# Expert weights read with 4 KB per partition instead of 1 KB and 2 KB rows, in a mixture-of-experts kernel

## The reference, cut to what matters

```python
xn = layernorm(x)                                   # 8192 tokens x 512
out = x + random_feature_attention(xn) + moe(xn)

# moe, E = 64 experts, CAP = 256 slots each, K = 8 experts per token, I = 256
dispatch[flat_e, pos_c] += tokens[tidx] * valid     # (64, 256, 512)
g = einsum('ech,ehi->eci', dispatch, gate_w)        # gate_w (64, 512, 256)
u = einsum('ech,ehi->eci', dispatch, up_w)          # up_w   (64, 512, 256)
expert_out = einsum('eci,eih->ech', silu(g) * u, down_w)   # down_w (64, 256, 512)
output[tidx] += expert_out[flat_e, pos_c] * weight
output += (silu(tokens @ sgate) * (tokens @ sup)) @ sdown  # the shared expert
```

## Time and profile before

| what | value |
|---|---|
| median of 3 runs | 1535.04 us (1531.94 to 1538.73) |
| the profiled execution, its own time | 1536.14 us |
| its span, first to last instruction | 1534.4 us |
| PE busy | 1405.3 us, 92% of the span |
| DVE, ACT, POOL busy | 863.6, 643.0, 538.4 us |
| DMA, mean over the span | 163 GB/s, 249.70 MB in 174406 packets |

### The profile page before, as it was taken

The page is one execution under the profiler, slowest core; times in us unless marked ns, Lnnn a source line. Parts: engine busy times, 40 slices in busy tenths (PEclk is TensorE's granted clock), DMA queues, the critical chain, the costliest instruction groups (busy, mean ns, idle before and its releaser), DMA issues.

```text
span 1534.4 us, 23572 instructions
## 1 busy us (share of the span) xinstructions
PE 1405.3 (92%) x7965; PEld 1179.7 (77%) x7965; DVE 863.6 (56%) x1700; ACT 643.0 (42%) x1004; POOL 538.4 (35%) x679
## 2 busy tenths in 40 slices
PE   7999999999999999999999978988898988889894
PEld 5677777777777777777778978887787888788783
DVE  6846565455654556555446655655565655555551
ACT  5321122211222112221145756666665656656562
POOL 2100000000000000000015776677767677677673
PEclk9999999999999999999999999999999999999997
DMA  7333122331223312232128988899898988988985
GB/s 252 124 120 115 61 74 96 114 114 55 78 96 114 114 48 84 96 114 87 47 73 243 277 242 234 235 247 250 227 253 230 256 237 228 270 215 235 259 230 64
DMA packets 174406, 249.70 MB, mean 163 GB/s; under 512 B 31268, under 2 KB 99880, under 8 KB 174376
## 3 DMA queue, kind: packets, MB, share of 16 engines
q1 hardware_dynamic: 145704, 177.99, 36.1%
q0 software_dynamic: 28672, 71.32, 20.7%
HBM read 177.88 MB, written 71.39 MB: 162 GB/s over the span
## 4 chain that ended last, share of the span: by engine, by line
PE 41%; DMA 28%; POOL 11%; issue 9%; DVE 8%; ACT 1%; POOLq 1%; SPq 0%; DVEq 0%
DMA out_dram<-outs,sidx 28%; PE pmm L994 8%; PE pmm L995 7%; PE pmm L996 7%; POOL out_dram L1362 5%; PE pout L994 4%; PE pout L995 4%; PE pout L996 4%; POOL sidx L1357 2%; PE plog L1062 2%; PE ptr L1006 2%; POOL earlier L1341 2%; PE pmm L1027 2%; DVE score L705 2%; POOL pool_sink L1288 2%
## 5 line engine op out<-in xcount | busy, mean ns | idle before, releaser
L994 PE MATMUL pmm<-xt_hi,proj_hi 128*128 128x256 f32 (+1 forms) x784 | 266.1, 339 | 3.9 <-DVE xt_lo L949 2.1
L1341 POOL TENSOR_TENSOR earlier<-earlier,chosen 128x64 bf16<-128x64 bf16 x64 | 28.5, 446 | 677.2 <-DVE chosen L734 673.4
L995 PE MATMUL pmm<-xt_lo,proj_hi 128*128 128x256 f32 (+1 forms) x784 | 256.8, 327 | 0.0
L996 PE MATMUL pmm<-xt_hi,proj_lo 128*128 128x256 f32 (+1 forms) x784 | 256.3, 327 | 0.0
L994 PE MATMUL pmm<-xt_hi,sgu_hi 128*128 128x256 f32 (+1 forms) x768 | 252.6, 329 | 0.1
L995 PE MATMUL pmm<-xt_lo,sgu_hi 128*128 128x256 f32 (+1 forms) x768 | 245.8, 320 | 0.0
L996 PE MATMUL pmm<-xt_hi,sgu_lo 128*128 128x256 f32 (+1 forms) x768 | 245.6, 320 | 0.0
L1362 POOL DMA_INDIRECT out_dram<-outs,sidx x128 | 216.4, 1691 | 33.9 <-issue 33.9
L448 ACT ACTIVATE feat<-pmm,ab 128x512 f32<-128x512 f32 x68 | 46.8, 689 | 386.3 <-PE pmm L1027 382.1
L994 PEld LDWEIGHTS pmm<-xt_hi,proj_hi 128*128 128x128 f32 x784 | 155.6, 199 | 26.2 <-issue 11.3
L1348 POOL DMA_INDIRECT xbuf<-rows,gidx x128 | 162.9, 1272 | 29.5 <-issue 28.5
(11 more groups left out here) (186 smaller groups left out, 2912.8 us busy)
## 6 DMA issues: line engine op xcount, KB each, us to landing
raw<-in_L_ffn_gate_w_dram SPq DMA_DIRECT2D x64, 512.0 KB
raw<-in_L_ffn_up_w_dram SPq DMA_DIRECT2D x64, 512.0 KB
raw<-in_L_ffn_down_w_dram SPq DMA_DIRECT2D x64, 512.0 KB
xbuf<-in_L_attn_x_dram SPq DMA_DIRECT2D x16, 1024.0 KB, 6.4
rows<-xn SPq DMA_DIRECT2D x16, 1024.0 KB, 4.2
outs<-in_L_attn_x_dram SPq DMA_DIRECT2D x32, 512.0 KB, 3.8
out_dram<-outs SPq DMA_DIRECT2D x32, 512.0 KB, 3.0
rows<-weight SPq DMA_DIRECT2D x16, 128.0 KB, 2.9
```

The costliest lines, as they stand in the source:

```text
L994: pe.matmul(psum, lh, rh, start=first and n == 0, stop=False)
L995: pe.matmul(psum, lh, rl, start=False, stop=False)
L996: ins = pe.matmul(psum, ll, rh, start=False, stop=final and n == len(pairs) - 1)
L1341: pool.tensor_tensor(after, earlier[b][:, j, :], chosen[:, j, :], ALU.add).then_inc(earlier_made, 1)
```

## The change

The weights of the 64 experts are laid into the partitions differently: partition `p` now gets rows `4p` to `4p+3` of gate and of up, and rows `2p` and `2p+1` of down. In DRAM these rows are neighbours, so that each partition takes one run of 4096 bytes per matrix, where it took four runs of 1024 (gate, up) or two of 2048 (down). The rest follows from that:

- the transposes of the tokens take every fourth column (`h:H:HB`, a step of 16 bytes) instead of 128 neighbouring ones, so that block `h` holds the token's columns `4p + h`;
- the columns of gate and up must come out so that output partition `q` of block `i` is column `2q + i`, since the down matrix holds rows `2q + i` in partition `q`. ACT and DVE therefore read `raw` with a step of 8 bytes (`egu_raw`) and write the high and low parts in neighbouring columns. The matmuls read what they read before;
- the shared expert keeps the old layout and gets a load function of its own.

The number and the order of the instructions, the waits and the bytes moved are the same on every engine.

```diff
+        egu_raw = [raw[b][:, 0:GU].rearrange("p (a q i) -> p a i q", q=P, i=IB) for b in range(2)]

             def load_gate_up(b, gate, up):
+                sp.dma_start(raw[b][:, 0:GU // 2], gate.rearrange("(p c) i -> p (c i)", p=P)).then_inc(
+                    gu_loaded[b], 16)
+                sp.dma_start(raw[b][:, GU // 2:GU], up.rearrange("(p c) i -> p (c i)", p=P)).then_inc(
+                    gu_loaded[b], 16)
+
+            def load_down(b, down):
+                sp.dma_start(raw[b][:, GU:], down.rearrange("(p c) h -> p (c h)", p=P)).then_inc(dn_loaded[b], 16)
+
+            def load_shared(b):
                 sp.dma_start(raw[b][:, 0:GU // 2].rearrange("p (c i) -> p c i", c=HB),
-                             gate.rearrange("(c p) i -> p c i", p=P)).then_inc(gu_loaded[b], 16)
+                             sgate_w.rearrange("(c p) i -> p c i", p=P)).then_inc(gu_loaded[b], 16)
...
             def gate_up_hi(e):
...
-                act.activation(egu_hi[e.b], raw[e.b][:, 0:GU], copy).then_inc(egu_hi_made, 1)
+                act.activation(egu_hi[e.b].rearrange("p (a i q) -> p a i q", i=IB, q=P), egu_raw[e.b],
+                               copy).then_inc(egu_hi_made, 1)
...
             def gate_up_lo(e):
                 dve.wait_ge(egu_hi_made, e.n + 1)
-                dve.tensor_tensor(egu_lo[e.b], raw[e.b][:, 0:GU], egu_hi[e.b].bitcast(F32),
+                dve.tensor_tensor(egu_lo[e.b].rearrange("p (a i q) -> p a i q", i=IB, q=P), egu_raw[e.b],
+                                  egu_hi[e.b].bitcast(F32).rearrange("p (a i q) -> p a i q", i=IB, q=P),
                                   ALU.subtract).then_inc(egu_lo_made, 1)
...
-                        ins = pe.transpose(ptr_e[:, h, c * P:(c + 1) * P], xe[e.b][:, c, h * P:(h + 1) * P],
+                        ins = pe.transpose(ptr_e[:, h, c * P:(c + 1) * P], xe[e.b][:, c, h:H:HB],
                                            ident[:])
```

More of the change, by code:

```diff
@@ L319, in load_gate_up @@
             def load_gate_up(b, gate, up):
+                sp.dma_start(raw[b][:, 0:GU // 2], gate.rearrange("(p c) i -> p (c i)", p=P)).then_inc(
[5 more added lines that the diff above has]
+            def load_shared(b):
                 sp.dma_start(raw[b][:, 0:GU // 2].rearrange("p (c i) -> p c i", c=HB),
-                             gate.rearrange("(c p) i -> p c i", p=P)).then_inc(gu_loaded[b], 16)
+                             sgate_w.rearrange("(c p) i -> p c i", p=P)).then_inc(gu_loaded[b], 16)
                 sp.dma_start(raw[b][:, GU // 2:GU].rearrange("p (c i) -> p c i", c=HB),
-                             up.rearrange("(c p) i -> p c i", p=P)).then_inc(gu_loaded[b], 16)
-            def load_down(b, down):
+                             sup_w.rearrange("(c p) i -> p c i", p=P)).then_inc(gu_loaded[b], 16)
                 sp.dma_start(raw[b][:, GU:].rearrange("p (c h) -> p c h", c=IB),
-                             down.rearrange("(c p) h -> p c h", p=P)).then_inc(dn_loaded[b], 16)
+                             sdown_w.rearrange("(c p) h -> p c h", p=P)).then_inc(dn_loaded[b], 16)
             def store_xn(g):
@@ L378, in _ @@
             sp.dma_start(router_raw, router_w.rearrange("(c p) e -> p c e", p=P)).then_inc(router_loaded, 16)
-            load_gate_up(0, sgate_w, sup_w)
-            load_down(0, sdown_w)
+            load_shared(0)
             sp.wait_ge(consts_made, 1)
```

## The result

| | before | after |
|---|---|---|
| median | 1533.79 us, 20 runs (1529.08 to 1543.63) | 1542.41 us, 20 runs (1531.89 to 1549.92) |
| the profiled execution, its own time | 1536.14 us | 1536.34 us |

The ratio is **1.0045**, 95% interval 1.0024 to 1.0065: the changed kernel is 0.45% slower, some 7 us. I had predicted 1508 us, and gave no change within 0.5% a chance of 0.24 and slower than that one of 0.20. The measured effect lies just inside that bound of 0.5%, and its interval reaches over it. It isn't the gain of 27 us that I worked out, and even its sign is the other one.

The account below looks back on a forecast made before the run. The expert stage's scatter-add loop, with weight loads on its chain, was taken as the bound. 59 turns x 0.55 us x 0.85 = 27.6 us off 1536.1 us, with the median 1.1 us lower, gave 1508 us; range 1484 to 1552 us.

Parts of the forecast that it names:

- The loop and its period: Expert stage: successive scatter-add pairs, with POOL's work between, form the bounding chain, 59 turns of 11.26 us each.
- The saving of the weights: Weight loads on the DMA engines: 4 KB packets save 0.55 us per turn, bounds 0.34 and 0.82 us.
- the rule that I had put aside: DMA transfers of 512 bytes and more already reach line rate; by it the saving on 1 KB rows would be 0.
- What of it reaches the end: Share of the weights' saving that shortens the scatter-add loop: 85% kept, 27.6 us over 59 turns.
- the room to the next bound: PE has 9.92 us of work per turn of 11.26 us, leaving 1.3 us before it bounds some turns.
- rival 3: DMA engines: scatter-adds stand behind longer weight packets, kernel slower, 1610 us or 1556 us with half of them; chance 0.12.
- Rival 3's decision point: Scatter-add pair, 16 packets per engine: rival 3 decides once 5 of them each wait behind a whole weight packet.
- The argument against rival 3: One traced microsecond shows weights served first while a scatter-add waits, so longer packets can't make it wait more.
- The strides: Strided reads: transposes 0.3 us of PE per turn, nothing on the chain; ACT and DVE reads unchanged.
- rival 2: Strided transposes make PE the bound: mild form 1524 to 1535 us, chance 0.13; dear form 1653 us, chance 0.06.
- Rival 1: Longer packets bring nothing: DMA engines cut them up, or the time given up is idle; 1535 us, chance 0.17.
- a clock that comes back with shorter waits: PE's clock, 0.96 in the expert stage and 1.00 in the dense one, would recover; reason for the range's 1484 us end.

Follow-up runs that it names:

- e7: Kernel before, with SP asking for the next expert's gate and up ahead of its wait for this expert's down tile: 1508.98 us, ratio 0.9841.
- e19: Kernel before plus one unused 512 KB load of gate per expert, in 4 KB runs: 1563.59 us, ratio 1.0190.
- e5: Kernel before, leaving out three of the four rows of up in each partition (384 KB per expert): 1513.21 us, ratio 0.9862.
- e6: Same cut of up as e5, with gate and down in 4 KB runs and unstrided reads: 1512.75 us, ratio 0.9866 to the kernel before.
- e4: Kernel before with gate and up in 2 KB runs, down as before, unstrided reads: 1535.53 us, ratio 1.0014.
- e1: Kernel before with only the 4 KB loads of the change, reads of ACT, DVE and transposes unstrided: 1541.93 us, ratio 1.0043.
- e18: Kernel before plus one unused 512 KB load of gate per expert, in 1 KB runs: 1551.29 us, ratio 1.0124.
- e16: e7 with gate and up in 2 KB runs and transposes at a step of 8 bytes: 1509.67 us, ratio 0.9847 to the kernel before.

## Why the prediction was wrong

**The loop and its period: right.** The chain of scatter-adds is the bound before and after the earlier trace rows, and in e7 and e19 the time moved together with the waits for flights and gathers.

**The saving of the weights, "0.55 us per turn": the sign was right, the size too large.** Over 661 us and 60.6 experts' worth of bytes (95.45 MB at 1.573 MB each) 46.8% is 5.10 us per expert; after, 94.54 MB at 43.5% make 4.78 us. The saving is 0.32 us, just under my lower bound of 0.34 us. I should have taken the gathers' row as it stood: it was the only measured long packet. The trace agrees here more with the rule that I had put aside than with my sum. The Trainium skill ("DMA: Bandwidth & Descriptors", Specifications) has line rate from 512 bytes on; 1 KB rows move at 343 GB/s, and those of 4 KB, from 1013 to 1014 us after, at 352 GB/s:

```profile
DMA packets 98, 0.35 MB, mean 352 GB/s; under 512 B 12, under 2 KB 12, under 8 KB 98
...
q1 hardware_dynamic: 98, 0.35, 104.1%
```

**The first step that failed: "What of it reaches the end ... I keep 85%".** e5 shows 29%. I had read the room to the next bound, 1.3 us on PE, as a wall that single turns hit now and then. It isn't PE alone: in e5 and e6 POOL's instructions, the gathers and PE take over shares of the chain as soon as the flight shortens. The sum with the measured terms is 59 x 0.32 x 0.29 = 5.5 us: at best 1528 us, not 1508. The 29% comes from a cut four times as large as this saving, and e4 says that it is still too much for a small one. By the same working e4 saves 0.28 us per expert (44.5% for 95.90 MB), 4.8 us at the end, and its interval excludes more than 1 us. Either less than 29% of a small saving arrives, or runs of 2 KB cost something too.

**The second step that failed: the sum has no term for what long packets cost the other queue.** That was rival 3, which I gave 0.12, and its effect is there at a far smaller size: e1 is 6.4 us over before, and if 5.5 us were gained the long packets cost about 12 us, 0.2 us per turn. This is what is left over, not a measurement of its own; at least the 6.4 us are measured. I had put the price at 1.8 us of flight per turn, or half of that. e19 against e18 confirms the sign with another load: 12 us net for one long load of 512 KB, where e1 loses 6.4 us net with three of them, so the size isn't a constant per packet. Rival 3's decision point ("from 5 packets of the 16") took every such wait to reach the end in full, nearly as the forecast did with the saving; by e5 some 29% of it does. Its mechanism, each packet of q0 behind a whole packet of q1, is not borne out: before, q1 sent nearly three packets for each of q0.

**The argument against rival 3 kept its term out of the sum:** "what has been waited for wholly can't be waited for more". The earlier trace rows is one microsecond in which the weights had nearly everything. From 1048 to 1051 us the same kernel has 291 packets of q0 beside 113 of q1: there the scatter-adds and gathers were served beside the weights, and in such stretches they get through 11% less after the change (0.117 instead of 0.132 MB per microsecond). One turn isn't the loop.

**The strides: right for this order, with a wrong reason in part.** I had called ACT's read free; it is 9% longer. (Its pattern is also cut into runs of 128, which no run tried by itself.) The transposes' load is half as long again (213 for 141 ns); that is 0.07 us per transpose, where rival 2 decides from 0.17 us, and the wait for gathers covers it, as the text had it. The Trainium skill ("SBUF — State Buffer", SBUF cachelines) has full rate only with two hits in a line of 16 bytes; the transposes, with one hit, are slower as it says, but so are ACT and e16's transposes (209 ns) with two, and DVE with two is not. Rival 2 as a bound on PE didn't come: PE still waits 71.4 us for gathers.

**Rival 1**, which had no change at the end, is what runs of 2 KB (e4) show: they free the engines and bring nothing that can be measured. Its second reason fits both kernels, since the time given up by the weights became idle time of the engines.

**The range**, 1484 to 1552 us, holds the median of 1542.41 us only because it reached into rival 3's mild case. At its lower end I had counted on a clock that comes back with shorter waits. It did not in e7, where they are shorter: 0.95 from 829 to 1470 us, against 0.96 in the earlier trace rows. Of what I had said would show it, three things came out against me: flights no shorter with fewer packets on q1, transposes that load in more than 200 ns, and a slower copy on ACT. (The sum itself, less its 1.1 us, is 1507.4 us, which I had written as 1508.)

## What to carry to other kernels

Where two DMA queues share the engines, longer packets on one can slow the other, even when they hold the engines for less time: before background loads are made longer, look at what flies beside them, and count it over the whole loop rather than in one turn. A saving on a resource that the chain waits for should be multiplied by a measured share. One kernel that simply leaves out a quarter of the load gives a first value for it in one run; a smaller saving can bring less, as e4 did. The order in which requests are made was worth more here than their shape: asking for the next weights ahead of a wait that doesn't concern them gave 1.6%.

## What the runs showed of the hardware that I had not expected

- In single microseconds with the engines full, packets of 1 KB moved at 343 GB/s and those of 4 KB at 352: nearly nothing is left to gain above 1 KB for a load that is alone.
- Two busy queues on the same engines share their time and not their packets: q1 held 48% in the mean, with 129 packets beside 46 of q0 per microsecond before and 40 beside 42 after. Single stretches differ widely (335 and 346 packets in 4 us of e18, 291 and 113 in 3 us of before). Beside packets of 4 KB, q0 moved 11% fewer bytes in such stretches.
- A read of 128x2048 float32 at a step of 8 bytes, in runs of 128, costs ACT 9% (1.93 to 2.10 us) and DVE nothing (2.29 us). The load of a 128x128 float32 transpose takes 213 ns instead of 141 at a step of 16 bytes, and in e16 209 ns at a step of 8 bytes.
- The effects of longer loads don't add: one of three 4 KB loads changes between -0.33% and +0.09%, two +0.3%, all three +0.43%. Why is open.
